# The last router's logits computed inside the output projection, a gather tile by tile and results given back tile by tile, in a two-layer transformer kernel

## The reference

```
x = layernorm(x + attention0(x))     # 16 heads of 16
x = layernorm(x + moe0(x))           # 8 dense experts, gates of the top 2
x = layernorm(x + attention1(x))     # 16 heads of 128, 4 groups of keys; ctx @ w_dense
x = layernorm(x + moe1(x))
```

## Time and profile before

| | |
|---|---|
| median of 3 runs | 892.85 us |
| profiled execution, its own time | 893.67 us |
| its span in the trace | 891.8 us |
| mean granted clock of PE | 0.988 |
| busy: PE / DVE / ACT / POOL | 817.7 / 693.9 / 496.5 / 391.0 us |
| chain that ended last | PE 71%, DVE 13%, issue 5%, DMA 3%, ACT 3%, POOL 3% |

### The profile page before, as it was taken

One profiled execution on the slowest core, in us unless ns is written; L12 is line 12 of the kernel. 1 busy time (PEld: TensorE's weight loads), 2 busy tenths in 40 slices (PEclk: granted clock), 3 DMA queues, 4 the chain that ended last, 5 costly groups with the idle time before them and its releaser, 6 DMA issues.

```text
span 891.8 us, 21987 instructions
## 1 busy us (share of the span) xinstructions
PE 817.7 (92%) x8131; PEld 514.1 (58%) x8227; DVE 693.9 (78%) x1921; ACT 496.5 (56%) x1181; POOL 391.0 (44%) x731
## 2 busy tenths in 40 slices
PE   7899999997898988979999999999999999997894
PEld 2455555553454544445566767666767766685374
DVE  4777777777688887678999888888888888856535
ACT  3577677765544534456666555656555565532243
POOL 4555667552365664523333343333333333333454
PEclk9999999999999999999999999999999999998998
DMA  5353333420000000016766565565556655550502
GB/s 167 107 127 91 94 84 97 121 31 8 2 1 1 1 1 1 1 28 122 119 123 123 97 104 104 99 101 98 96 99 103 104 105 97 97 91 1 95 1 95
DMA packets 219034, 67.70 MB, mean 76 GB/s; under 512 B 211360, under 2 KB 214704, under 8 KB 218928
## 3 DMA queue, kind: packets, MB, share of 16 engines
q1 hardware_dynamic: 218928, 66.29, 37.4%
HBM read 17.92 MB, written 4.19 MB: 25 GB/s over the span
## 4 chain that ended last, share of the span: by engine, by line
PE 71%; DVE 13%; issue 5%; DMA 3%; ACT 3%; POOL 3%; SPq 0%; POOLq 0%; DVEq 0%; ACTq 0%
PE bank L469 15%; PE bank L470 14%; PE bank L468 13%; PE bank L601 4%; PE bank L836 4%; PE bank L838 4%; PE bank L837 4%; DVE nm L1439 3%; DMA att<-w_lo 2%; PE bank L548 2%; PE bank L543 2%; PE bank L524 2%; PE bank L585 1%; DVE w_lo L1463 1%; DVE scr L1614 1%
## 5 line engine op out<-in xcount | busy, mean ns | idle before, releaser
L1157 ACT ACTIVATE att<-att,nm 128x512 f32<-128x512 f32 (+3 forms) x256 | 141.5, 553 | 104.4 <-DVE nm L1452 103.0
L1062 ACT ACTIVATE scr<-bank 128x512 bf16<-128x512 f32 (+3 forms) x210 | 111.5, 550 | 86.5 <-PE bank L838 44.2
L469 PE MATMUL bank<-w_lo,scr 128*128 128x256 bf16 (+1 forms) x478 | 144.0, 301 | 0.5
L468 PE MATMUL bank<-w_hi,scr 128*128 128x256 bf16 (+1 forms) x471 | 141.5, 300 | 2.9 <-DVE scr L1381 1.9
L470 PE MATMUL bank<-w_hi,scr 128*128 128x256 bf16 (+1 forms) x476 | 143.2, 301 | 0.1
L1439 DVE TENSOR_REDUCE nm<-bank 128x1 f32<-128x512 f32 (+3 forms) x256 | 110.6, 484 | 37.9 <-PE bank L548 37.8
L2070 POOL TENSOR_SCALAR wqkv_hi<-att,rr 128x512 bf16<-128x512 f32 (+3 forms) x128 | 66.1, 536 | 136.2 <-DVE rr L1469 136.2
L1452 DVE CUSTOM_DVE_ANT_0 att<-bank,consts 128x512 f32<-128x512 f32 (+3 forms) x256 | 113.2, 483 | 14.9 <-PE bank L470 14.9
L1108 ACT ACTIVATE att<-bank 128x512 f32<-128x512 f32 (+1 forms) x192 | 90.8, 528 | 50.1 <-PE bank L585 49.7
L1381 DVE TENSOR_TENSOR scr<-bank,scr 128x256 bf16<-128x256 f32 (+1 forms) x146 | 77.4, 540 | 51.0 <-ACT scr L1062 50.6
L2070 POOL TENSOR_SCALAR w_hi<-att,rr 128x512 bf16<-128x512 f32 (+3 forms) x128 | 66.1, 535 | 106.2 <-DVE rr L1469 106.2
(11 more groups left out here) (242 smaller groups left out, 2014.7 us busy)
## 6 DMA issues: line engine op xcount, KB each, us to landing
scr<-wall_in SPq DMA_DIRECT2D x19, 512.0 KB, 4.7
v_by_token<-scr SPq DMA_DIRECT2D x16, 128.0 KB, 1.8
scr<-v_by_token SPq DMA_DIRECT2D x16, 128.0 KB, 3.5
x_tok<-x_tok_in SPq DMA_DIRECT2D x4, 512.0 KB, 5.1
scr<-x_t_in SPq DMA_DIRECT2D x3, 512.0 KB, 5.7
out<-x_tok SPq DMA_DIRECT2D x3, 512.0 KB, 2.6
scr<-wqkv_in SPq DMA_DIRECT2D x2, 384.0 KB, 3.6
att<-w_hi SPq DMA_TRANSPOSE x32, 3.4
```

The costliest lines, as they stand in the source:

```text
L468: pe.matmul(out, l_hi, r_hi, start=start, stop=False, skip_group_check=check)
L469: pe.matmul(out, l_hi, r_lo, start=False, stop=False, skip_group_check=check)
L1062: return act.activation(out, in_, ACT.Copy)
L1157: last = act.activation(at, at, ACT.Exp, bias=nm[:, j % 2, qt:qt + 1], scale=-1.0, accum_out=rs[:, j % 2, qt:qt + 1])
```

## The change

**The router inside the projection.** The last router is centred (its mean over the 256 features is taken off each expert's column), so that the mean which a layer norm subtracts falls out of the logits; the positive factor of the norm changes no choice and is applied only for the probabilities. `w_dense @ router` is computed once: 32 DMA transposes turn the high and low parts of `w_dense`, PE multiplies them by the centred router between steps of the mix (two heads a tile in `FOLD_AT`), and DVE writes the result as eight more columns of each head's block, which is 264 wide now. Each projection matmul has 264 columns, and six more add the residual's part. The turned tiles, their copies and `last_logits` are gone. The exponential is taken once, late.

**The end of attention 1.** The last four tiles' logits are copied from the projection's banks. PE adds the residual to those banks by an f32 matmul with the identity (`add_rows`); DVE measures there, between the choices; POOL makes four deviations at once and ACT norms the tiles into `x_tok`.

**Gather and give-back.** Both halves are gathered tile by tile for tiles 0 to 11, then k = 0 and k = 1 of the last four. The first filler block is gone and the second goes to another bank. `give_back` finishes one tile after the other, and the shared tiles are 1, 3, 5, 7, 9.

The diff, cut to its core:

```diff
-SHARED = (1, 4, 7, 10, 13)
-JOINED = (0, 2, 3, 5, 6, 8, 9, 11, 12, 14, 15)
-MEASURES = (0, 2, 3, 1, 5, 6, 4, 8, 7, 9, 11, 10, 12, 14, 13, 15)
+SHARED = (1, 3, 5, 7, 9)
+JOINED = (0, 2, 4, 6, 8, 10, 11, 12, 13, 14, 15)
+MEASURES = (0, 2, 1, 4, 3, 6, 5, 8, 7, 10, 9, 11, 12, 13, 14, 15)
...
-WP, OUTW, EXPW, WQ, WKV, WD, W1, W2 = 0, 512, CH, 5 * CH, 9 * CH, 11 * CH, 15 * CH, 17 * CH
+WP, OUTW, EXPW, WQ, WKV, WD, W1, W2 = 0, 512, CH, 5 * CH, 9 * CH, 11 * CH, 15 * CH + HEADS * NX, 17 * CH + HEADS * NX
+DW = E + NX
+DENSE_CHUNKS = range(11, 15)
+MEAN_AT, FOLD_AT = 1, range(6, 14)
...
+    sp.wait_ge(ch_done, NCH)
+    sp.wait_ge(a["pv"], 3 * NT)
+    for hd in range(HEADS):
+        for part, w in enumerate((w_hi, w_lo)):
+            sp.dma_start_transpose(wd_t[part][:, KE * hd:KE * (hd + 1), :], w[:, ds(WD + hd * DW, E)]
+                                   ).then_inc(ld_fold, 16)
...
+    def router_mean():
+        for i, part in enumerate((rw_hi, rw_lo)):
+            for k in range(KE):
+                last = pe.matmul(bank[3][:, E:DW], ones_b[:, :], part[:, 1, k * NX:(k + 1) * NX],
+                                 start=(i == 0 and k == 0), stop=(i == 1 and k == KE - 1), skip_group_check=True)
+        last.then_inc(e["mean"], 1)
+    def fold_router(heads):
+        pe.wait_ge(ld_fold, 16 * 2 * HEADS)
+        for hd in heads:
+            for k in range(KE):
+                ks = slice(k * NX, (k + 1) * NX)
+                last = mm3(bank[3][:, E + hd * NX:E + (hd + 1) * NX], wd_t[0][:, hd * KE + k, :],
+                           wd_t[1][:, hd * KE + k, :], router_hi[:, ks], router_lo[:, ks], k == 0, k == KE - 1, True)
+        if heads[-1] == HEADS - 1:
+            last.then_inc(e["fold"], 1)
     def second_project(t):
         pe.wait_ge(m["tlo"], TURNS.index(("cm", t)) + 1)
         hold(pe, m["r2"], t)
+        if t == MEAN_AT:
+            router_mean()
+        if t == MEAN_AT + 1:
+            pe.wait_ge(e["router"], 1)
+        if t in FOLD_AT:
+            first = 2 * FOLD_AT.index(t)
+            fold_router(range(first, first + 2))
+        if t == FOLD_AT[-1] + 1:
+            pe.wait_ge(e["folded"], 1)
         project(bank[3][:, 0:E], tc_hi[t % 2], tc_lo[t % 2], OUTW).then_inc(m["o2"], 1)
...
             cs = ds(cb + hd * TOK, P)
-            ws = slice(WD + hd * E, WD + (hd + 1) * E)
-            last = mm3(out, ct_hi[:, cs], ct_lo[:, cs], w_hi[:, ws], w_lo[:, ws], hd == 0, hd == HEADS - 1)
+            ws = slice(WD + hd * DW, WD + (hd + 1) * DW)
+            last = mm3(out, ct_hi[:, cs], ct_lo[:, cs], w_hi[:, ws], w_lo[:, ws], hd == 0, hd == HEADS - 1, True)
+            if hd == 0:
+                for k in range(KE):
+                    xs, ks = ds((g - TT) * P, P), slice(k * NX, (k + 1) * NX)
+                    mm3(out[:, E:DW], xt_hi[:, k, xs], xt_lo[:, k, xs], router_hi[:, ks], router_lo[:, ks],
+                        False, False, True)
         return last
...
         hold(pe, c["clo"], HEADS * (g // TT) - (HEADS // 2 if part == 0 else 0))
         if part == 0:
             hold(pe, c["od"], g - TT + 1)
-        last = dense_heads(bank[7][:, 0:E], g, range(part * HEADS // 2, (part + 1) * HEADS // 2))
+            hold(pe, e["lgc"], g - TT)
...
+    def add_rows(t):
+        pe.matmul(bank[DENSE_BANKS[t % TT]][:, 0:E], ident_f, x_tok[:, t * E:(t + 1) * E], start=False, stop=True,
+                  skip_group_check=True).then_inc(e["sum"], 1)
...
                 pe.wait_ge(e["ylo"], i // 2 + 1)
             back = chosen_t[:, t * TOK + i * P:t * TOK + (i + 1) * P]
             pe.matmul(out, back, y_hi[:, i * E:(i + 1) * E], start=(i == 0), stop=False)
...
     pe.wait_ge(c["max"], 3 * NH)
+    iota_rows()
     last_dense(DONE + 2, 0, 12)
     l1_pv(NT - 1, 2)
-    hold(pe, c["kvl"], 2 * NT)
     last_dense(DONE + 1, 0, 13)
...
-    last_turn(DONE + 3)
-    last_logits(DONE + 2)
-    last_logits(DONE + 3)
-    pe.wait_ge(e["lgc"], DONE + 1)
-    keep_busy(FILL, bank[1])
+    pe.wait_ge(e["lgc"], NT)
+    for t in range(DONE, NT):
+        add_rows(t)
     ranks()
-    keep_busy(FILL, bank[1])
+    keep_busy(FILL, bank[6])
+    for t in range(DONE):
+        for k in range(KE):
+            gather(k, t)
     for k in range(KE):
-        for t in range(NT):
+        for t in range(DONE, NT):
             gather(k, t)
...
-            give_back(t, parts)
-    for t in range(TT, NT):
-        give_back(t, range(TT))
+    for t in range(NT):
+        give_back(t)
...
-    last_high(DONE - 1)
     rows_high(2)
-    router_exp(e, 1, slice(0, DONE * NX))
     l1_context_high(NT - 1, 3)
-    for t in range(DONE, NT):
-        last_high(t)
-    router_exp(e, 2, slice(DONE * NX, NT * NX))
-    rows_high(3)
     act.wait_ge(e["cnt"], 1)
     copy(count_b, bank[5][:, 0:2 * P]).then_inc(e["cntb"], 1)
+    act.wait_ge(c["rstd"], DONE + 1)
+    for t in range(DONE, NT):
+        act.activation(x_tok[:, t * E:(t + 1) * E], bank[DENSE_BANKS[t % TT]][:, 0:E], ACT.Identity,
+                       bias=shift_t[:, t:t + 1], scale=rstd_x[:, t:t + 1]).then_inc(e["xn"], 1)
+    act.wait_ge(e["xn"], TT)
+    copy(row_hi[:, DONE * E:NT * E], x_tok[:, DONE * E:NT * E]).then_inc(e["rhi"], 1)
+    act.wait_ge(e["scaled"], 1)
+    act.activation(powers, scaled, ACT.Exp).then_inc(e["ex"], 1)
     act.activation(shift_t[:, 0:1], one_f[:, 0:1], ACT.Gelu).then_inc(e["rhi"], 1)
     for k in range(KE):
         act.wait_ge(e["buf"], k + 1)
-        copy(xt_hi[:, k, 0:TOK], bank[(4, 6)[k]][:, :]).then_inc(e["bhi"], 1)
+        copy(xt_hi[:, k, 0:TOK], bank[(3, 6)[k]][:, :]).then_inc(e["bhi"], 1)
...
                           rcc[:, b * HEADS:(b + 1) * HEADS, q:q + 1].to_broadcast([P, HEADS, D0]), ALU.mult
                           ).then_inc(m["cc"], 1)
+    def center_router():
+        dve.wait_ge(e["mean"], 1)
+        chain = Chain(dve, e["dve"], 0)
+        for k in range(KE):
+            ks = slice(k * NX, (k + 1) * NX)
+            chain(dve.scalar_tensor_tensor(router_f[:, ks], bank[3][:, E:DW], -1.0 / E, rw_f[:, 1, ks],
+                                           ALU.mult, ALU.add))
+        chain(dve.tensor_copy(router_hi[:, :], router_f[:, :]))
+        dve.tensor_tensor(router_lo[:, :], router_f[:, :], router_hi[:, :], ALU.subtract).then_inc(e["router"], 1)
+    def folded():
+        rows = bank[3][:, E:E + HEADS * NX].rearrange("p (h c) -> p h c", c=NX)
+        dve.wait_ge(e["fold"], 1)
+        dve.tensor_copy(dense_rows(w_hi)[:, :, E:DW], rows).then_inc(e["fhi"], 1)
+        dve.wait_ge(e["fhi"], 1)
+        low(dense_rows(w_lo)[:, :, E:DW], rows, dense_rows(w_hi)[:, :, E:DW]).then_inc(e["folded"], 1)
     def joined(t, which):
         rows = x_tok[:, t * E:(t + 1) * E]
         slot = 2 * (which - 1) + t % 2
         dve.wait_ge(m[f"o{which}"], t + 1)
+        if which == 2 and t == MEAN_AT:
+            center_router()
+        if which == 2 and t == FOLD_AT[-1]:
+            folded()
...
     def l1_join(t):
         rows = x_tok[:, ds(t * E, E)]
-        i = max(0, t - DONE)
+        i = 0
         hold(dve, c["o"], t + 1)
-        dve.tensor_tensor(rows, bank[7 if t < DONE else DENSE_BANKS[t % TT]][:, 0:E], rows, ALU.add
-                          ).then_inc(c["od"], 1)
+        dve.tensor_tensor(rows, bank[7][:, 0:E], rows, ALU.add).then_inc(c["od"], 1)
+        dve.tensor_copy(lg[:, t, :], bank[7][:, E:DW]).then_inc(e["lgc"], 1)
...
         chain(dve.tensor_reduce(r1c[:, 2, ts], lg[:, ts, :], AX.X, ALU.max))
-        dve.tensor_tensor(row(0), lg[:, ts, :], wide(2), ALU.subtract).then_inc(e["lgd"], 1)
-        dve.wait_ge(e["lgd"], turn)
+        chain(dve.tensor_tensor(row(0), lg[:, ts, :], wide(2), ALU.subtract))
         chain(dve.scalar_tensor_tensor(row(4), row(0), 0.0, rev[:, ts, :], ALU.is_equal, ALU.mult))
         chain(dve.tensor_reduce(r1c[:, 2, ts], row(4), AX.X, ALU.max))
         chain(dve.tensor_tensor(first[:, ts, :], rev[:, ts, :], wide(2), ALU.is_equal))
-        dve.wait_ge(e["ex"], turn)
-        chain(dve.scalar_tensor_tensor(row(3), first[:, ts, :], -2.0, row(1), ALU.mult, ALU.add))
...
-    l1_join(DONE)
-    l1_join(DONE + 1)
-    l1_norm(DONE)
-    l1_join(DONE + 2)
-    l1_norm(DONE + 1)
-    last_low(DONE)
-    l1_join(DONE + 3)
-    l1_norm(DONE + 2)
-    last_low(DONE + 1)
-    l1_norm(DONE + 3)
-    last_low(DONE + 2)
-    last_low(DONE + 3)
-    dve.wait_ge(e["lg"], DONE + 1)
-    dve.tensor_copy(lg[:, DONE:NT, :], bank[6][:, 0:TT * NX].rearrange("p (t x) -> p t x", x=NX)
-                    ).then_inc(e["lgc"], 1)
-    dve.wait_ge(e["lgc"], DONE + 1)
+    for t in range(DONE, NT):
+        dve.wait_ge(c["o"], t + 1)
+        dve.tensor_copy(lg[:, t, :], bank[DENSE_BANKS[t % TT]][:, E:DW]).then_inc(e["lgc"], 1)
+    dve.wait_ge(e["lgc"], NT)
...
-    for t in range(2 * TT):
+    def deviation(t):
+        i, rows = t - DONE, bank[DENSE_BANKS[t % TT]][:, 0:E]
+        dve.wait_ge(e["sum"], i + 1)
+        dve.bn_stats(stats[:, i, :], rows).then_inc(c["st"], 1)
```

(38 more changed lines are left out.)

146 lines of the change are left out of this document (44 added, 102 removed).

## The result

The changed kernel took 881.12 us in the median of five runs (878.32 to 881.62), the kernel before 892.11 beside it: ratio 0.9862, 95% interval 0.984 to 0.9885, so about 12.3 us less (10.3 to 14.3) by the ratio and 11.0 by the medians. The forecast was 9.9 less, with 880.3 to 887.0 as the range. Repeated in another series the ratio was 0.9888 (0.9862 to 0.9915), 881.03 against 891.03 us, 10.0 less.

The account below looks back on a forecast made before the run. TensorE was taken to bound the mix nearly and the attention groups fully, a chain over engines the end. Terms +2.65 + 0.6 - 7.6 - 1.05 - 4.5 = -9.9 gave 883.8 us, median 883.0, range 880.3 to 887.0.

Parts of the forecast that it names:

- The sum: Whole kernel: terms give -9.9 us, taking the profiled 893.67 to 883.8, or 883.0 for the median.
- The mix: Expert mix: router centring 0.45 us and 100 small matmuls 2.2 us, partly covered by waits; +2.65 us.
- The transposes: 32 DMA transposes issued on SP, about 1.35 us each, landed by 285 us, hidden by 26 us of slack; cost nothing.
- The attention groups: Attention groups with output projection: wider matmuls +2.6, small logit matmuls +0.6, turned tiles gone -2.6; +0.6 us (-1 to +1.5).
- To the choice: Last projection to first choice of slots: logits copied at 814.08 instead of 821.68, later 6.07 us unchanged; -7.6 us.
- The gather: First choice to copy of the second half: one unbroken tile-by-tile run, 14.35 us instead of 15.42; -1.05 us, 0.25 slack.
- GpSimd's four-wide chain 1.92 (872.12 to 874.04): In the gather: GpSimd's chain for the last four tiles' rows taken as 1.92 us, rows ready at +10.6, needed at +10.85.
- The give-back: Final stage: first tile added at 867.05 instead of 868.21, shared tiles over earlier; -4.5 us (-5 to -2.5).
- The clock: Rival in the ranking: TensorE's clock falls, gather +2.75 us and ranks +0.5, 886.3 us; chance 0.12.
- GpSimd's order: Rival in the give-back: GpSimd's chains between shares hold VectorE's measures, -2.3 instead of -4.5, 885.2 us; chance 0.13.
- Late transposes: Rival at the sixth projection: TensorE stands for transposes that land late, +35 us, about 918 us; chance 0.04.
- unshortened chain: Rival before the choice: logits' copy waits for something else, about -2 instead of -7.6, 888.6 us; chance 0.04.

Follow-up runs that it names:

- e2: The changed kernel run again with no edit; 881.03 us, ratio 0.9888 to the kernel before.
- e4: The changed kernel with the 96 small fold matmuls moved to where TensorE waits for VectorE in steps 7, 8 and 11; mix 125.50 us, ratio 0.9862 to the kernel before.
- e10: The changed kernel with VectorE waiting after choice 5 until GpSimd's chain of four is done; gather 15.75 us, span 883.5 us.
- e3: The changed kernel without the 32 transposes and 96 small matmuls, folded columns filled from a constant; median 878.92 us, mix 125.54 us.
- e8: The kernel before with only the first twelve tiles' gather done tile by tile; gather 14.57 us, ratio 0.9995.
- e5: The kernel before with results given back tile by tile, shared tiles left at 1, 4, 7, 10, 13; ratio 1.0001.
- e7: The kernel before with both the tile-by-tile give-back and shared tiles 1, 3, 5, 7, 9; ratio 0.995.
- e6: The kernel before with shared tiles at 1, 3, 5, 7, 9, give-back order unchanged; ratio 0.9944.
- e11: The changed kernel without its remaining block of filler matmuls behind the ranks; gather 16.14 us against 15.13, span 879.8 us.

## Where the prediction was right, and where it was wrong

**The sum, and the step that failed.** Put together from the stages, leaving out the start: mix +1.96; attention groups +1.25 (means of the seven executions with the fold, 444.68, and of the six with the kernel before's code there, 443.43); to the first choice -7.98; gather -0.29; to the last norm -4.46; the last output -0.14. That is -9.7, and the forecast was -9.9; the repeat, e2, measured -10.0. In part that is luck: against the measured stages I had the mix 0.7 and the choice 0.4 too long, the gather 0.8 and the attention groups 0.65 too short, and these errors cancel.

The first result lay lower, 879.8 by its ratio, under the range's end of 880.3. The step that failed is "The profiled execution took 893.67 us (span 891.8 and 1.87 around it): 883.8", with the range round it. It carried one execution's time over to the changed kernel with a term of nothing for the 245 us ahead of the mix, and the range was made of the other terms' bounds alone. Instead, the mix began 1.84 us earlier in the profiled pair, and the attention stretch was 0.9 below the changed kernel's mean. Before's execution had the latest start of the fourteen (244.93). Under the same code the start moves by 4.6 us (239.86 in e4, 244.46 in e10; the two don't differ ahead of the mix), by the landing of the constants and by TensorE's clock, as e2 shows.

**The mix,** forecast +2.65, was +1.96. The term took 0.45 us for the router and one of eight steps with cover. The router cost 0.20 (e3), and cover stood in two steps, 1.76 instead of 2.2. What I missed is larger: the waits in rows 2 could have taken it all; e4 needs three of the six. I counted instructions against stages and not against places.

**The transposes,** put at nothing, were hidden where I looked: issue 1.25 us each against my 1.35, the last at 278 us. Where I did not look they were not free, see next.

**The attention groups,** +0.6 (-1 to +1.5), were +0.25 in the first pair of profiles and +1.25 in the means, and not for my reasons. I put the wide projection at +0.6 and the transposes at nothing. e3 has the wide projection without the fold: 443.25, inside the 443.05 to 443.74 of the kernel before's code. The seven with the fold have 443.75 to 445.65. So the projection costs nothing that shows, and the fold, whose transposes have landed 90 us before these groups begin, goes with +1.3. About 0.9 of it is time in which TensorE waits for the DMA transposes of the probabilities: 3.9 to 4.6 us without the fold (e3: 4.04), 4.4 to 6.2 with it, and in part at other places of the stretch. One of them, 0.89 us in e10:

```profile
546.13 0.23 PE L890 MATMUL bank<-att,w_hi 128*128 128x128 bf16 x1 [0.89 <-DMA att<-w_lo]
```

How 32 earlier transposes come to move these waits was not tried, and e3 is a single execution. Matmuls of 264 columns start 0.112 us apart, as forecast.

**To the choice,** -7.6, was -7.98: the copy came 0.32 us after the last projection matmul's start, against 0.31, and the chain behind it took 5.68 instead of 6.07, as TensorE's ranks no longer ran at the low clock; one small reduction of VectorE's (L1829) also left the chain, and the two were not taken apart. I had the clock as a danger and not as a gain: rows 8 showed that before already paid for it.

**The gather,** -1.05, was -0.29. The failed step is "GpSimd's four-wide chain 1.92 (872.12 to 874.04)", moved from a place where VectorE ran other operations to one where it chooses: 2.75 there, and 2.04 when VectorE stood still from the second operation on (e10). A duration taken from another neighbourhood was used unchanged, in a term with 0.25 us of slack. The remaining 0.2 is the latency of the first gather and copy (14.57 in e8 against 14.35).

**The give-back,** -4.5, was -4.46 in size and wrong in parts: I had 1.15 us from the first add, and it is worth 0.2 alone (e5) and nothing beside the new shares (e7). The rest came from the shared tiles alone (e6). That the size came out is luck, as two errors met: VectorE, no longer held, takes in the late start, so that the early one adds nothing to it.

**The rivals.** The clock falls only without the filler (e11: +1.0 of the 2.75 priced). GpSimd's order binds in e5, which has the old shares, and not after the change. Late transposes and an unshortened chain did not come.

## What to carry to other kernels

Put small extra matmuls where the engine already waits for another one, not in front of the work that they belong to: 96 of them cost 1.8 us in one place and nothing in another. Before an earlier start is counted as a gain, follow the loop over engines to the end of the stage, and see whether anything in it waits for a step that itself waits for the loop. Work that is hidden where it runs can still cost later, so compare the stages behind it too. And judge parts by distances between fixed points of the program: the same code moved the start by 4.6 us, and four of the distances behind it agree to 0.1.
